# Attention scores and maxima as 64-row products on the two row halves of TensorE's array, with q used where its projection leaves it

## What is computed

```python
q = t @ Wq.T + bq        # t: group-normed x as tokens, 1024 per image
k = t @ Wk.T + bk
v = t @ Wv.T + bv        # in the reference 8 heads of 64 channels
q = q.reshape(B * NUM_HEADS, S, hd)   # a group: 128 consecutive tokens, 1024 rows of 64
scores = jnp.einsum('gqd,gkd->gqk', q, k) / jnp.sqrt(hd)
attn = jax.nn.softmax(scores, axis=-1)
wv = jnp.einsum('gqk,gkd->gqd', attn, v)
x = x + wv               # laid back as channels
# layer 1: x + conv3x3(relu(mask(group_norm(x)) * group_norm(x))) + bias
```

## Time and profile before

| | |
|---|---|
| median of 3 runs | 2581.28 us (2579.69 to 2582.69) |
| profiled execution, its own time | 2579.7 us |
| its span, first to last instruction | 2577.9 us |
| TensorE products busy | 2501.4 us (97%) |
| TensorE weight loads | 987.6 us (38%) |
| VectorE busy | 1939.5 us (75%) |
| ScalarE busy | 1141.6 us (44%) |
| GpSimd busy | 1128.4 us (44%) |

### The profile page before, as it was taken

One profiled execution on the slowest core, in us unless ns is written; L12 is line 12 of the kernel. 1 busy time (PEld: TensorE's weight loads), 2 busy tenths in 40 slices (PEclk: granted clock), 3 DMA queues, 4 the chain that ended last, 5 costly groups with the idle time before them and its releaser, 6 DMA issues.

```text
span 2577.9 us, 39692 instructions
## 1 busy us (share of the span) xinstructions
PE 2501.4 (97%) x11720; PEld 987.6 (38%) x11720; DVE 1939.5 (75%) x2647; ACT 1141.6 (44%) x2059; POOL 1128.4 (44%) x971
## 2 busy tenths in 40 slices
PE   6999999999999999999999999999999999999999
PEld 2333333333333333333333333333344444444444
DVE  5887787778788787777878798976866966967515
ACT  4455555555545545555555554556232132132100
POOL 1366566556546746655664664655112021030000
PEclk9999999999999999999999999999999999999999
DMA  5234153242433315333342533332434634633534
GB/s 159 72 84 119 62 130 85 68 123 62 116 97 100 98 47 139 86 92 104 78 119 64 133 96 84 104 89 86 174 144 145 248 131 169 239 131 131 196 108 170
DMA packets 209915, 301.71 MB, mean 117 GB/s; under 512 B 82208, under 2 KB 131488, under 8 KB 209696
## 3 DMA queue, kind: packets, MB, share of 16 engines
q1 hardware_dynamic: 209424, 297.97, 38.9%
q10 hardware_dynamic: 272, 1.05, 0.1%
HBM read 195.54 MB, written 52.69 MB: 96 GB/s over the span
## 4 chain that ended last, share of the span: by engine, by line
PE 86%; DVE 5%; issue 2%; DMA 2%; ACT 1%; SPq 1%; POOL 1%; DVEq 0%; ACTq 0%; POOLq 0%
PE bank L846 29%; PE bank L752 16%; PE bank L726 14%; PE bank L687 11%; PE bank L705 8%; PE bank L697 6%; DVE nmax L1280 2%; PE bank L715 1%; DMA q_b<-shift 1%; DVE prob_sum L1274 1%; ACT prob L929 1%; PE bank L739 1%; SPq L419 1%; DVE qk_lo L1266 1%; DMA den_col<-den_sb 0%
## 5 line engine op out<-in xcount | busy, mean ns | idle before, releaser
L1280 DVE TENSOR_REDUCE nmax<-bank 128x1 f32<-128x512 f32 x1024 | 657.9, 682 | 231.7 <-PE bank L705 227.4
L929 ACT ACTIVATE prob<-bank 128x512 f32<-128x512 f32 x1024 | 560.7, 593 | 496.9 <-PE bank L726 492.5
L846 PE MATMUL bank<-v,u_slab 128*128 128x512 f16 x3456 | 746.9, 379 | 0.0
L1109 POOL TENSOR_TENSOR prob_sum<-prob_sum,prob 128x512 f32<-128x512 f32 x354 | 502.7, 1420 | 370.2 <-ACT prob L929 369.2
L752 PE MATMUL bank<-prob,val 128*64 128x512 f32 x2048 | 496.6, 606 | 0.0
L846 PEld LDWEIGHTS bank<-v,u_slab 128*128 128x128 f16 x3456 | 338.1, 98 | 407.0 <-issue 0.8
L705 PE MATMUL bank<-k_a,q_a 128*128 128x512 f16 x1024 | 384.2, 383 | 14.5 <-DVE nmax L1280 6.8
L1274 DVE TENSOR_TENSOR prob_sum<-prob_sum,prob 128x512 f32<-128x512 f32 x354 | 357.7, 1011 | 3.5 <-issue 0.3
L726 PE MATMUL bank<-q_a,k_a 128*128 128x512 f16 x1024 | 315.5, 381 | 16.6 <-ACT prob L929 15.0
L726 PE MATMUL bank<-q_b,k_b 128*128 128x512 f16 x1024 | 305.6, 380 | 9.0 <-DMA q_b<-shift 8.9
L752 PEld LDWEIGHTS bank<-prob,val 128*64 128x64 f32 x2048 | 124.3, 136 | 248.5 <-issue 206.4
(11 more groups left out here) (142 smaller groups left out, 2588.1 us busy)
## 6 DMA issues: line engine op xcount, KB each, us to landing
u_slab<-u_scratch SPq DMA_DIRECT2D x72, 1024.0 KB, 5.0
xs<-x SPq DMA_DIRECT2D x28, 1024.0 KB, 5.6
tile<-x_scratch SPq DMA_DIRECT2D x26, 1024.0 KB, 6.9
u_scratch<-u_w SPq DMA_DIRECT2D x96, 192.0 KB, 2.8
q_a<-qk_hi SPq DMA_DIRECT2D x64, 256.0 KB, 4.8
den_sb<-recip_scratch SPq DMA_DIRECT2D x128, 128.0 KB, 2.9
x_scratch<-xr SPq DMA_DIRECT2D x16, 1024.0 KB, 4.6
xr<-x SPq DMA_DIRECT2D x15, 1024.0 KB, 7.6
```

The lines of the kernel that those rows point to most:

```text
L846: mm = pe.matmul(bank_at(pos, co)[:].rearrange("p (i n) -> p i n", i=2), slab[:, l, c, co * P:(co + 1) * P], image[v][:, 2 * c:2 * c + 2, ...
L929: act.activation(prob[:, (2 * u + e) % 8], sc_bank[bank_turn(s * 16 + 2 * u + e, 16 * HPI)[0]][:], ACT.Exp, scale=float(D) ** -0.5).then_i ...
L1109: nc.gpsimd.tensor_tensor(acc, in0, prob[:, (2 * kc + 1) % 8], ALU.add).then_inc(s1["sum1"], 1)
L1280: dve.tensor_reduce(nmax[:, m // 2, m % 2:m % 2 + 1], src[:], AX.X, ALU.max, negate=True)\
```

## The change

- Scores: each of the two 128-row products of a score tile becomes two 64-row products. The two tiles of a unit (`e` = 0, 1) use the upper and the lower 64 rows of the array and alternate, so that eight products stand where four stood. The fourth of each tile takes an array of eights (`eights`) and `q_top`, which is zero but for the shift in rows 0 and 64.
- Maxima: 16 products of 128 rows (q hi twice against k hi and k lo) become 16 of 64 rows (q hi against k hi), in 8 pairs, one product on each row half, into two ring banks taken together. `MAX_AT` has them at places `a` and `c`; place `b` is gone.
- Projections, weights times v and denominators are unchanged.
- ScalarE and VectorE write q and k, hi and lo, straight into arrays of the right half image (`q_hi`, `q_lo`, `k_hi`, `k_lo`). q needs no copy. Of k, the two segments of a tile are copied once to the other row half (`move_k`, four transfers instead of six for k and six for q).
- The shift goes out in two transfers instead of one.
- In the last image's slots, VectorE copies the denominator (`den_from_bank`) ahead of unit 1's maximum items as before.

```diff
-MAX_QUOTA = [2, 3, 3, 3, 3, 2, 0, 0]
+MAX_AT = {(0, "a"): 0, (1, "a"): 1, (2, "a"): 2, (2, "c"): 3, (3, "a"): 4, (4, "a"): 5, (4, "c"): 6, (5, "a"): 7}
...
-            def move_qk(which, t, half, first=False):
-
-                sp.wait_ge(s1["qk_split"], 2 + 8 * t + 4 * (which + 1))
...
+            def move_k(t, half):
+
+                sp.wait_ge(s1["qk_split"], 2 + 8 * t + 4)
+                for v in (k_hi, k_lo):
+                    for e in range(2):
+                        sp.dma_start(v[half][(1 - e) * D:(2 - e) * D, NC:SEG], v[half][e * D:(e + 1) * D, 0:NC])\
+                            .then_inc(s1["qk_moved"], 16)
...
-                sp.dma_start(q_b[half][D:D + 1, :, tok], shift[:]).then_inc(s1["shift_row"], 16)
+                for e in range(2):
+                    sp.dma_start(q_top[half][e * D:e * D + 1, :, tok], shift[e::2]).then_inc(s1["shift_row"], 16)
...
-            def max_tile(s, m):
+            def max_pair(s, n):
 
                 half, tok = tokens(s)
-                dst = take()
-                pe.matmul(dst[:].rearrange("p (k t) -> p k t", t=TOK), q_a[half][:, m // 2, tok],
-                          k_a[half][:, 4 * (m % 2):4 * (m % 2) + 4, tok],
-                          start=True, stop=True).then_inc(s1["ring_full"], 1)
+                dst = take(), take()
+                part = n % 2
+                for e in range(2):
+                    rows = slice(e * D, (e + 1) * D)
+                    pe.matmul(dst[e][:].rearrange("p (k t) -> p k t", t=TOK), q_hi[half][rows, n // 2, tok],
+                              k_hi[half][rows, NC * part:NC * part + NC, tok],
+                              start=True, stop=True).then_inc(s1["ring_full"], 1)
...
             def scores(h, s, u, part):
...
-                k_op, q_op = ((k_a, q_av), (k_b, q_bv))[part]
                 for e in range(2):
                     b, ago = bank_turn(s * 16 + u * 2 + e, 16 * HPI)
                     if part == 0:
                         pe.wait_ge(s1["exp_done"], 16 * h + 2 * u + e + 5 - ago)
...
+                for n in (2 * part, 2 * part + 1):
+                    for e in range(2):
+                        b, _ = bank_turn(s * 16 + u * 2 + e, 16 * HPI)
+                        rows = slice(e * D, (e + 1) * D)
+                        at = u // 2 + NC * ((u + e) % 2)
+                        k_op = (k_hi[half][rows, at, tok], k_lo[half][rows, at, tok], k_hi[half][rows, at, tok], eights[rows])[n]
+                        q_op = (q_hi, q_hi, q_lo, q_top)[n][half][rows, :, tok]
+                        mm = pe.matmul(sc_bank[b][:].rearrange("p (j t) -> p j t", t=TOK), k_op, q_op,
+                                       start=(n == 0), stop=(n == 3))
+                        if n == 3:
+                            mm.then_inc(s1["scores_full"], 1)
...
-                        pe.wait_ge(s1["qk_moved"], 192 * (t + 2))
+                        pe.wait_ge(s1["qk_moved"], 64 * (t + 2))
+                        pe.wait_ge(s1["qk_split"], 2 + 8 * (t + 2))
                     run("a")
                     scores(h, s, u, 0)
-                    run("b")
                     if u == 0:
-                        pe.wait_ge(s1["shift_row"], 16 * (h + 1))
+                        pe.wait_ge(s1["shift_row"], 32 * (h + 1))
                     scores(h, s, u, 1)
                     run("c")
...
-            for m in range(16):
-                max_tile(0, m)
-                if m % 4 == 1:
-                    project_qk(1, 1, 0, m // 4)
+            for n in range(SEG):
+                max_pair(0, n)
+                if n % 2 == 0:
+                    project_qk(1, 1, 0, n // 2)
...
-            for v in (k_b[1], q_b[1]):
-                dve.memset(words(v)[D:P], 0.0).then_inc(s1["kb_clear"], 1)
```

110 lines of the change are left out of this document (45 added, 65 removed).

## The result

The kernel after takes 2626.46 us (median of 4 runs, 2624.4 to 2633.23), the kernel before beside it 2581.04 (4 runs, 2579.69 to 2582.69): a ratio of 1.018, 95% interval 1.0161 to 1.02. The forecast was 2581, so it is 45 us too low, and the time lies above the range of 2540 to 2605. The profiled execution took 2624.4 us, its span 2622.4.

The account below looks back on a forecast made before the run. The prediction took TensorE, busy 97% of the span, as the bound overall. Its terms, -8.4 + 0 + 1.5 + 6.5 + 2.5 - 2 = +0.1 us, gave 2579.8 profiled and 2581 as median, range 2540 to 2605.

Parts of the forecast that it names:

- ScalarE's shadow: Slots 3 and 7: maxima hidden in TensorE's wait for ScalarE save nothing; +0.4 together for each of 15, 6.5 us.
- The q and k slots: Slots 0, 1, 4, 5: -1.73 maxima, +0.76 shape changes, +0.63 ring waits; -0.4 taken for slots 0, 4, 5, -8.4 us.
- Slots 1: Eight slots where VectorE also has the moments, busy 25.5 of 30.4, so unit 4's pair starts late; 0 taken.
- The value slots: Slots 2 and 6: -1.73 + 0.76 + 1.77 - 0.68 = +0.12 us, +0.1 taken; fifteen slots, +1.5 us.
- The ring's 1.77 - 0.68: Value slots: pairs wait 1.77 us for banks in units 2 and 4, while two earlier ring waits, 0.68, go.
- Copies, start and tail: k's copies leave before q is made, -2 us; first slot and last image's four slots without projection, +2.5 us.
- A pair is one product: Score and maximum products: two 64-row products on different row halves together take 0.216 us, like one 512-column product.
- rival 3: All 40 pairs of a slot: a row pair costs more than one product; 10 ns each gives 2603; chance 0.14.
- rival 5: All pairs: the row halves don't overlap, 8.6 us per slot in 45 slots; +500, 3080 us; chance 0.07.
- The changes of shape: Projection edges: changing between 128 rows and row halves costs 0.09 us each way, 0.76 us per slot, 34 us.
- rival 2: Projection edges: changing between 128 rows and row halves is free; -34 us, 2547; chance 0.20.
- Rival 4: Slots 0, 1, 4, 5: VectorE 0.5 us behind at second pairs, ring starves TensorE; +29 or less, 2595 to 2610; chance 0.09.

Follow-up runs that it names:

- run 1: The kernel after with TensorE's loop over six images written out, so that it takes no jump backwards: 2600.52 us, ratio 1.0088.
- run 2: The kernel before with TensorE's loop over six images written out: 2574.17 us, ratio 0.9981.
- run 5: The kernel after with 96 idle semaphore instructions at TensorE's start, where it waits for input: 2602.26 us, ratio 1.0097.
- run 12: The kernel after with 32 idle semaphore instructions at TensorE's start: 2614.24 us.
- run 13: The kernel after with 64 idle semaphore instructions at TensorE's start: 2604.34 us.
- run 15: After with 96 idle instructions, denominators' copy first, pairs moved in projection slots, and VectorE's last split in slots 3 and 7 put in unit 6: 2580.97 us, ratio 1.0008.
- run 6: The kernel after with 96 idle instructions at TensorE's start and VectorE's denominators' copy ahead of its first sum in unit 2: 2594.0 us, ratio 1.0055.
- run 7: The kernel after with 96 idle instructions at TensorE's start and VectorE's maxima over 256 of 512 columns: 2546.68 us, ratio 0.9862.
- run 9: The kernel before with VectorE's maxima over 256 of 512 columns: 2555.34 us, ratio 0.9905.
- run 4: The kernel before with 64 idle semaphore instructions ahead of TensorE's loop: 2592.2 us.
- run 3: The kernel after with 96 idle semaphore instructions ahead of TensorE's loop, behind the first head's work: 2614.95 us.

## Why the prediction was wrong

Two steps of the sum failed. It had no term for a stall of TensorE's instructions at the loop's jump, which cost the change 19 to 29 us; and it gave slots 3 and 7 no waits on the ring, where they and VectorE made a loss of 18.0 us out of the forecast 6.5. With the jump away on both sides the change still costs 26 us, so the forecast of no change fails by the second step as well; the first one took the time out of the range.

**The jump was not in it.** The sum had terms for slots, copies and the start, and none for TensorE's instruction stream, though the stalls of before can be read in its trace (0.8 to 1.6 us at five places, L705's idle time "issue 5.6" in the earlier trace rows) and though the diff puts eight products where four stood, 2048 more on each of PE and PEld. Shown by runs 1, 2, 5, 12 and 13. Slots 0 and 1 of after lost 34.1 us to it (28.0 + 6.1 against run 1), those of before 4.9 (against run 2): 29.2 of the 44.6. By the medians of the same runs it is 19.1 (45.4 - 26.35), since the written-out loop makes the kernel after longer elsewhere, in slots 3, 4, 5 and 7.

**No ring term in slots 3 and 7.** The prediction gave them +0.4 each for ScalarE's shadow and nothing for the ring, and says nothing on why. They lost 1.23, over the run 18.0 instead of 6.5 (15 times 0.41 is 6.2). The shadow was sized right: with half reductions 0.41 and 0.42. The rest is VectorE, in the slot in which it is busy 93%. Two operations of it fell between a pair and the next one: the split in unit 0 (run 15, 0.4) and the sum held up by GpSimd in unit 2 (run 6, 0.2 in slots 3 and 0.66 in slots 7).

**The q and k slots**: forecast -0.4, measured -0.34 and -0.33 in slots 4 and 5. Its terms: -1.73 + 0.76 = -0.97 where run 7 against run 9 has -0.87, and a ring of 0.63 where it is 0.54. So here the mechanism was right. **Slots 1**: forecast 0; without the jump +0.6 in the middle pass (30.33 in run 1, 29.73 in run 2), 4.4 us over eight slots; what of VectorE's work makes it, no run tells.

**The value slots**: forecast +0.12, measured +0.27 in slots 6 and +0.1 for all slots 2 together. The ring's 1.77 - 0.68 was too much: by runs 7 and 9 it is 1.00 after and 0.54 before. With half reductions slots 6 stand only 0.19 under before (29.26, 29.45) and not 0.97, but 0.53 us of idle time are left in them (29.26 - 28.73), so that the two terms aren't told apart there.

**Copies, start and tail**: forecast -2 for the copies; the first copy came 2.4 earlier. Forecast +2.5 for the first slot and the last image's slots 4 to 7; these four lost 2.2 (they are in the sums of their kinds).

**A pair is one product**: 0.216, as forecast, so rivals 3 and 5 fell. Four pairs of slot 3 from 625.05 on, kernel after:

```profile
625.05 0.39 PE L696 MATMUL bank<-k_hi,q_hi 64*128 64x512 f16 x2
...
625.92 0.38 PE L724 MATMUL bank<-q_top,spare 64*128 64x512 f16 x2
```

0.87 / 4 = 0.2175. To the nanosecond these starts are 625048, 625274, 625490, 625706 and 625922: 226 and then three times 216, and the 226 isn't the pairs' own, since single products too stand 225 to 227 ns apart in the first step behind a change of operation. So a pair costs no more than a single product. Slot 4 of run 7 stands 0.10 us over the forecast of its TensorE work, at most 2.5 ns for each of 40 pairs. The second product of a pair starts 3 or 4 ns behind the first, which agrees with the Trainium skill's 4 ns for each further tile (TensorE: Matmul & The Clock Gate, Part 3: Packing small matmuls); but the next pair isn't put off by it, so to add it once for each pair, as the prediction does beside its sum, is too much.

**The changes of shape** cost 0.09 each way, as forecast, and rival 2 fell. From a projection's last product to a pair it is 0.31 in the kernel after, and as much from a pair to a projection (566.99 to 567.30); the L750 group stayed at 1.94:

```profile
601.38 0.38 PE L685 MATMUL bank<-w_hi,xn_lo 128*128 128x512 f16 x1
601.69 0.39 PE L696 MATMUL bank<-k_hi,q_hi 64*128 64x512 f16 x2
```

**Rival 4** (the ring starves TensorE, 2595 to 2610, chance 0.09) was the right mechanism for what isn't the jump's: less the jump's share of 19.1 to 29.2 the kernel is at 2597 to 2607, inside its range. But that range was worked out for slots 0, 1, 4 and 5, and the waits stood in 3, 7 and 1, so the number is right by luck.

Where it balances at the last copy: jump 29.2, slots 3 and 7 18.0, slots 1 without the jump 4.4, slots 4 to 6 -4.7, slots 2 0.1, start -2.4, together 44.6.

## What to carry to other kernels

Count instructions as well as their time: an edit that makes a loop's body longer moves every jump and every position behind it. The row to look for is idle time put down to "issue" at the start of a loop's pass, and a second standstill some products behind it, whatever that one is put down to. Before judging such an edit, move the loop by a few dozen idle instructions, or write it out on that engine, in both kernels; here this moved one kernel by 24 to 26 us, as much as the edit itself costs with the jump away.

A saving on the busiest engine that concentrates its requests on another (two tiles at once instead of one and one) must be costed operation by operation on the other one, with whatever stands between two requests, and in the slots in which that engine is fullest first.

## What was not expected of the hardware

- At a jump back in TensorE's stream it goes on 2.5 to 3.1 us after the start of the packet of instructions, and where two packets start together 4.05 to 4.45 us after the second. What isn't hidden is idle: 0.8 to 1.6 us in the kernel before, 3.4 to 5.7 in the kernel after (both stalls of a jump together), 1.3 to 2.3 in the same kernel with 64 or 96 instructions in front of its loop. The granted clock falls behind the long ones: the eight L750 products take up to 3.78 us instead of 1.94.
- Instructions that only add to a semaphore keep TensorE idle for 7.61 us (64 of them, run 4) and 13.17 us (96, run 3), 0.12 and 0.14 us each, with a part hidden behind products already issued; in run 5 the first product starts at 15.77, put down to issue, 0.16 for each of 96. Run 3's first copy moved by 16.1 us, since products at half the clock follow.
- Two sums on VectorE and GpSimd that start 0.1 us apart go all but one after the other, and a shift of 0.2 us in when they start decides which of the engines pays: 0.68 or 1.71 us on VectorE, 1.73 or 1.27 on GpSimd.
